# Attention with absorbed keys: eight heads stream past one batch's queries, in two column halves of the array

## The reference, cut to what matters

```python
x = x + attn(cond(x, subjects, weights, bias), WA, bA, ...)     # 64 batches x 64 tokens x 512
x = x + ffn(cond2(x, ...), Wg, bg, W1, W2)                      # 4 experts, top 2, unchanged

# cond: einsum('bct,bcd->bdt', x, weights[subject]) + bias[subject]
# attn, NH = 16 heads, DH = 128, DHR = 64, L = 128:
h = x @ WA + bA;  kv_lat, q_lat = split(h, 2)                    # 128 + 128 features
kRt = rope(h @ WB + bB);  qRt = rope(h @ WC + bC)                # 64 shared; 64 for each head
q, k, v = q_lat @ WUQ, kv_lat @ WUK, kv_lat @ WUV                # 128 for each head
scores = (q . k + qRt . kRt) * (128 + 64) ** -0.5, causal
out = softmax(scores) @ v @ WZ + bZ
```

## Time and profile before

| | |
|---|---|
| runs | 2027.82, 2028.1, 2031.16 us; median 2028.1 |
| profiled execution | span 2027.3 us from its first to its last instruction |
| start to the first attention matmul (weights absorbed) | 0 to 45.8 us |
| attention, eight groups | 45.8 to 1041 us |
| routing | to about 1269 us |
| experts | to the end |
| one group of attention, from one `bias_rows` to the next | 123.2 us (535.8 to 659.0) |

### The profile page before, as it was taken

How to read it: one execution, slowest core, us unless ns; L and a number is a source line. 1 busy time by engine, 2 the same in 40 slices (tenths; PEclk the granted TensorE clock), 3 DMA queues, 4 the chain that set the end, 5 groups by cost and what they waited for, 6 DMA issues and landing times. The chain is left out here.

```text
span 2027.3 us, 29249 instructions
## 1 busy us (share of the span) xinstructions
PE 1936.4 (96%) x10616; PEld 1601.5 (79%) x10616; DVE 944.1 (47%) x1604; ACT 627.5 (31%) x1088; POOL 735.3 (36%) x541
## 2 busy tenths in 40 slices
PE   6999999999999999999979997999999999999996
PEld 4788888888888888888867776787877878787875
DVE  4664656556475654747532386323323232323311
ACT  4323323233232323323212311333323333333321
POOL 2222222322223222232200003557565665657563
PEclk9999999999999999999989999899999999999998
DMA  6000101000010100101032212404312330322011
GB/s 244 21 1 16 47 0 62 0 32 30 0 62 0 62 0 0 62 0 63 1 83 93 94 68 71 168 0 128 88 32 41 124 78 5 103 98 47 0 21 21
DMA packets 68646, 104.88 MB, mean 52 GB/s; under 512 B 11904, under 2 KB 29056, under 8 KB 68608
## 3 DMA queue, kind: packets, MB, share of 16 engines
q1 hardware_dynamic: 49024, 77.69, 11.0%
q0 software_dynamic: 7168, 16.78, 4.3%
q10 hardware_dynamic: 12416, 9.88, 1.6%
HBM read 79.18 MB, written 25.17 MB: 51 GB/s over the span
## 5 line engine op out<-in xcount | busy, mean ns | idle before, releaser
L1721 DVE CAST hh<-hid 128x512 fp32r<-128x512 f32 x128 | 72.5, 567 | 483.0 <-ACT hid L1666 479.9
L396 POOL TENSOR_TENSOR rope_cos<-rope_raw,table_attend 128x512 f32<-128x512 f32 x72 | 93.2, 1295 | 454.2 <-ACT rope_raw L459 425.3
L1596 POOL TENSOR_TENSOR w1l<-w_raw,w1h 128x512 fp32r<-128x512 f32 x112 | 179.3, 1601 | 163.9 <-ACT w1h L1658 154.7
L95 PE MATMUL e_h<-xh,w1h 128*128 (+1 forms) x512 | 204.2, 399 | 14.8 <-POOL w1l L1596 13.4
L95 PE MATMUL bank_o<-Mh,mix_h 128*128 128x512 f32 x512 | 210.8, 412 | 0.0
L97 PE MATMUL e_h<-xh,w1l 128*128 (+1 forms) x512 | 202.5, 395 | 0.0
L96 PE MATMUL e_h<-xl,w1h 128*128 (+1 forms) x512 | 202.4, 395 | 0.0
L97 PE MATMUL bank_o<-Mh,mix_l 128*128 128x512 f32 x512 | 201.8, 394 | 0.0
L96 PE MATMUL bank_o<-Ml,mix_h 128*128 128x512 f32 x512 | 201.7, 394 | 0.0
L95 PE MATMUL e_y<-w2h,hh 128*128 128x512 f32 x512 | 200.1, 391 | 0.4 <-DVE hl L1723 0.4
L97 PE MATMUL e_y<-w2h,hl 128*128 128x512 f32 x512 | 199.3, 389 | 0.0
(11 more groups left out here) (297 smaller groups left out, 4047.6 us busy)
## 6 DMA issues: line engine op xcount, KB each, us to landing
w_raw<-in_W_dram SPq DMA_DIRECT2D x56, 512.0 KB, 4.2
stage<-in_x_dram SPq DMA_DIRECT2D x8, 1024.0 KB, 7.2
x_res<-in_x_dram SPq DMA_DIRECT2D x8, 1024.0 KB, 5.0
out_dram<-x_res SPq DMA_DIRECT2D x32, 256.0 KB, 2.0
flat_dram<-flat_sb ACTq DMA_DIRECT2D x32, 256.0 KB, 2.0
rows<-out_dram SPq DMA_DIRECT2D x4, 1024.0 KB, 5.5
x_odd<-out_dram SPq DMA_DIRECT2D x4, 1024.0 KB, 6.2
stage<-in_W_dram SPq DMA_DIRECT2D x8, 512.0 KB
```

Of the source, the lines that this page charges most:

```text
L95: nc.tensor.matmul(out, ah, bh, start=start and n == 0, stop=False)
L396: nc.gpsimd.tensor_tensor(by_cos[:, :].rearrange("p (b t) -> p b t", b=GB), v, cos.unsqueeze(1).to_broadcast([P, GB, C]), ALU.mult).then_i ...
L1596: nc.gpsimd.tensor_tensor(w1l[:, k, :, :], w1_at(pair, chunk), w1h[:, k, :, :].bitcast(F32), ALU.subtract).then_inc(S["w1_lo"], 1)
L1721: nc.vector.tensor_copy(hh[:, k, :], hid[:, k, :]).then_inc(S["h_hi"], 1)
```

## The change

A head's product with A now goes to the keys: `absorb_weights` computes A transposed (operands of L285 swapped), and `keys_absorbed` makes A kv_lat for every head, in place of `q_nope_mm` (3 matmuls for each of 16 heads in both). A **unit** `i` is now eight heads (`hb = i // 4`) of two batches (`n = i % 4`); there are eight units a group as before. In `scores` a batch's 64 queries are the stationary operand, and the absorbed keys of eight heads, 512 columns, stream past it; the two batches write partitions 0 to 63 and 64 to 127 of one bank, with stationary operands of 64 columns each. The keys' rope part is kept block-diagonal (`kblk`), for two heads at a time.

`mix` has four matmuls of 256 columns. `wz` of a unit is a closed sum over eight heads in one bank `bank_o`, so `x2_tile` adds to the residual once for each unit. The conditioning bias moves through the latent projection (`colsum`, `latent_bias`); the residual is stored and reloaded by quarters.

```diff
-                    nc.tensor.matmul(bank_s[:, cols], q_nope[:, b, :, :].rearrange("p h t -> p (h t)"),
-                                     lat32[:, 0, cols], start=b == 0, stop=False)
-                pe.wait_ge(S["rope_done"], g * NR + u + 2)
-                for b in range(GB):
-                    cols = slice(b * C, (b + 1) * C)
-                    last = nc.tensor.matmul(bank_s[:, cols], q_rope[:, b, :, :].rearrange("p h t -> p (h t)"),
-                                            k_rope[:, cols], start=False, stop=b == GB - 1)
...
+                half = [slice(j * C, (j + 1) * C) for j in range(2)]
+                tok = [slice((2 * n + j) * C, (2 * n + j + 1) * C) for j in range(2)]
+                for j in range(2):
+                    nc.tensor.matmul(bank_s[i % 2][half[j], :], q32[:, tok[j]], kabs[:, :, tok[j]],
+                                     start=True, stop=False)
+                for u in range(UB):
+                    for j in range(2):
+                        last = nc.tensor.matmul(bank_s[i % 2][half[j], u * P:(u + 1) * P], q_rope[:, u, tok[j]],
+                                                kblk[:, 2 * n + j, :, :].rearrange("p h t -> p (h t)"),
+                                                start=False, stop=u == UB - 1)
...
+                for j in range(2):
+                    for h in range(2):
+                        rows = slice(h * C, (h + 1) * C)
+                        toks = slice(j * C, (j + 1) * C)
+                        last[h] = nc.tensor.matmul(bank_m[h][:, :].rearrange("p (u q) -> p u q", u=UB)[:, :, toks],
+                                                   kv_tok[rows, (2 * n + j - h) % GB, :], probT[rows, :, toks],
+                                                   start=True, stop=True)
...
+            def wz(g, i, heads):
...
+                    if k == 0:
+                        pe.wait_ge(S["mix0_lo"], g * STEPS + i + 1)
+                        pe.wait_ge(S["x2_ev"], g * STEPS + i)
...
+            def keys_absorbed(g, h):
+                if h % HB < 2:
+                    pe.wait_ge(S["raw_ev"], g * NR + h // HB * UB + 4 + h % HB)
+                else:
+                    pe.wait_ge(S["ka_ev"], g * NH + h - 1)
...
+            def turn(r, sin):
+
+                dve.wait_ge(S["raw_ev"], r + 1)
+                dve.wait_ge(S["rope_done"], r)
+                nc.vector.memset(wait_here[:, :], 0.0)
+                nc.vector.stream_shuffle(swapped[:, :], raw[:, :], [i ^ 1 for i in range(32)]
+                                         ).then_inc(S["swap_ev"], 1)
...
+            def q_raw(g, u):
+                act.wait_ge(S["qr_mm"], g * NU + u + 1)
+                act.wait_ge(S["swap_ev"], g * NR + u + 1)
+                act.wait_ge(S["cos_ev"], g * NR + u + 1)
...
+            pe.wait_ge(wa_in, 16)
+            pe.wait_ge(t_ev["k"], HG)
+            for i in range(2):
+                for c in range(TC):
+                    last = nc.tensor.matmul(bank_t["k"][:, 2 * i:2 * i + 2], wa[:, c, i * L:(i + 1) * L],
+                                            K.parts["ones"][:, 0:2], start=c == 0, stop=c == TC - 1)
```

More of the change, by code:

```diff
@@ L330, in attention @@
[L330 to L337, removed]
+        lat_bias = (raw, swapped)
@@ L341, in attention @@
+        xres_in = K.xres_in
+        x2_out = [sem(f"at_x2_out{k}") for k in range(2)]
         block = ctx.enter_context(nc.Block())
@@ L449, in kv_tokens @@
[L449 to L451 removed]
+                nc.scalar.copy(lat_h[:, i, :], lat32[i]).then_inc(S["lat_hi"], 1)
+            def kv_tokens(g, k):
+                act.wait_ge(S["kvt_mm"], g * 2 + k + 1)
+                nc.scalar.copy(kv_tok[:, 4 * k:4 * k + 4, :], bank_p[k][:, :].rearrange("p (n l) -> p n l", n=4)
                                ).then_inc(S["kvt_ev"], 1)
[L454 to L459 removed]
@@ L520, in body @@
                         cond_hi(g + 1, c)
-                    latent(g + 1, 0)
-                    latent(g + 1, 1)
-                    kv_tokens(g + 1)
-                    rope_raw((g + 1) * NR, S["kb_mm"], g + 2, bank_d, K["bB"][:, 0:1])
+                    latent_hi(g + 1, 0)
+                prob_transposed(g, 6)
+                if more:
+                    latent_hi(g + 1, 1)
+                mix_hi(g, 6)
+                if more:
+                    keys_raw(g + 1)
+                    for u in range(UB):
+                        q_raw(g + 1, u)
+                    for h in range(HB):
+                        keys_absorbed(g + 1, h)
+                prob_transposed(g, 7)
+                if more:
+                    exps(g + 1, 0)
+                mix_hi(g, 7)
+                if more:
+                    kv_tokens(g + 1, 0)
+                    kv_tokens(g + 1, 1)
+                    exps(g + 1, 1)
             over_groups(act, first, body)
@@ L656, in first @@
                 latent_lo(0, 1)
[L657 to L683 removed]
+                keys_rope(0)
@@ new lines, in first @@
+            def first():
+                bias_rows(0, first=True)
+                for c in range(TC):
+                    cond(0, c, first=True)
+                latent(0, 0)
+                latent(0, 1)
+                rope_keys(0)
+                for u in range(UB):
+                    q_rope_mm(0, u)
+                for h in range(HB):
+                    keys_absorbed(0, h)
+                scores(0, 0, first=True)
+                scores(0, 1, first=True)
+                kv_tokens(0)
```

833 lines of the change are left out of this document (446 added, 387 removed).

## The result

The changed kernel takes 1979.0 us (median of 4 runs, 1978.1 to 1983.4) against 2028.0 (4 runs, 2027.4 to 2031.2) on the same chip: a ratio of 0.9757, 95% interval 0.9742 to 0.9771. It is faster, by 49 us where 67 were forecast: 2 us above the forecast of 1945 to 1977, and within the range given.

The account below looks back on a forecast made before the run. PE was taken as the bound, busy 122.3 of 123.2 us a group. Terms of -9.9 us a group gave -79 for eight; clock +7 and edges +5 made -67: 1961 us, forecast 1945 to 1977, range 1931 to 2012.

Parts of the forecast that it names:

- Scores, -12.3 a group: PE's f32 score matmuls: with column halves fully overlapped, 1.95 us a unit against 3.49, -12.3 us a group.
- The bound that the weight loads would add time: Score matmuls: 20 loads of 64 columns not hidden, 1.1 us a unit, 70 us in all: 2031; chance 0.04.
- The rival of a partial overlap: Score column halves overlap only in part, a pair costing 1.25 of one, +28 us: 1989; chance 0.12.
- The serial rival: Score column halves (L878, L882) run one after the other, +112 us less 16 of hidden waits: 2057; chance 0.12.
- Returns to fp32r, -1.2: First fp32r matmul behind f32 ones costs 0.32 instead of 0.23; about 14 a group, not 27: -1.2 us.
- Waits, +4.1 in sum: PE's waits a group: -0.8 us for old ones that go, +3.9 for a new one, +1.0 for others.
- The seam, +3.9: Front of a group: PE waits for `rope_raw` before `keys_absorbed` 1, a 12.8 us chain against 9.0 of matmuls: +3.9 us.
- Other waits, +1.0: Two or three PE waits of 0.52 us a group around `wz`, mix, scores or transposes: +1.0, from 0 to 4.
- Transposes, +0.4: Four more PE transposes a group for `kv_tokens`: +0.4 us.
- Clock, +7: New PE wait at seven group boundaries brings half clock behind some, 4 x 1.7 us: +7, from 0 to 12.
- Edges, +5: First group's front, without `wz` to fill and with a longer DVE chain, +4 us; end of `absorb_weights`, +1.
- The rivals of small and of long waits: PE waits: small, 1.8 us a group and clock holds, 1930, chance 0.15; long, 3 us more a group, 1990, chance 0.12.

Follow-up runs that it names:

- the run with the halves apart: Changed kernel with all five score matmuls of the first column half issued before those of the second: 2050.3 us, ratio 1.0094.
- the second buffer and all moved: Changed kernel with `rope_raw` doubled, scores kept in the probabilities' place, both reorderings, and unit 0's residual addition ahead of a DVE rope step: 1941.7 us, ratio 0.9570.
- both reorderings: Changed kernel with PE's and DVE's order changed at the front of a group, PE's and ACT's in its middle: 1955.2 us, ratio 0.9627.
- a second buffer: Changed kernel with `rope_raw` given a second buffer, used in turn, and scores kept in the probabilities' place: 2000.4 us, ratio 0.9858.
- DVE's line alone moved: Kernel with a second buffer, unit 5's residual addition moved ahead of two rope steps in DVE's queue, PE's order unchanged: 2003.5 us, ratio 0.9864.
- the middle alone mended: Changed kernel reordered only in mid-group: the mix of unit 2 moved ahead of `keys_absorbed` 9, ACT's copies likewise: 1969.0 us, ratio 0.9704.

## Why the prediction was right, and where it was off

- *Scores, -12.3 a group.* Right, and for the reason given. The bound that the weight loads would add time did not come: 20 records a unit pass in two slots of 0.43 and eight of 0.11, though both halves share their rows. The rival of a partial overlap falls too: a pair costs 1.0 of one. The Trainium skill ("TensorE: Matmul & The Clock Gate", Part 3) measured 2.38 for three column tiles; the estimate of 1.26 for a pair that the prediction worked out from it does not agree with this trace of two. The serial rival falls as well, and the run with the halves apart shows that it was a true one: at 1.7 times the time of a pair the kernel is 0.9% slower than before. In proportion (71 us for 0.71) the 49 us of the measured gain are gone at about 1.5; the 1.6 of the prediction belonged to a gain of 67.
- *Returns to fp32r, -1.2.* Right: there are 26 returns before and 14 after, each 0.09 longer than 0.23, so -1.1 is there. Entries into halves cost nothing new: the last fp32r matmul takes 0.33 ahead of halves six times a group now; before it was eight times, all ahead of the mix. That the row of the fp32r matmuls moves by only -0.1 comes from the waits.
- *Waits, +4.1 in sum.* **This is the term that was most undersized.** Idle time grew by 4.4, near the forecast. But each of the four waits costs 0.27 more in the matmuls on its two sides, and two short stops under 0.15 us that the view does not list (527.07 to 527.74, 544.80 to 545.52) cost another 0.45 together: 1.5 us a group, against 0.5 ahead of the three waits of before. So waits are +5.4. A kernel with half as many such stops bears it out: with the second buffer and all moved, the fp32r matmuls without waits are 76.2 us a group instead of 77.0.
- *The seam, +3.9.* The forecast came from a chain of 12.8 us. The chain took 13.3 (from 523.14, where the keys' matmuls are through, to 536.44), so PE, with 9.0 us of its own to issue, lost 4.3, of which 3.4 are listed as idle, in three stretches instead of one or two. The 0.5 more is in the two additions for the keys: 2.39 us instead of 1.9, the second beside POOL's product of 527.43.
- *Other waits, +1.0.* The fourth wait, of 1.91 us in the middle of the group, was in no term by name; the 1.0 us were placed at mix, scores or `wz`. There ACT's copy (581.74) comes when POOL's cosine product ends, at 581.65, behind POOL's division and residual bias (578.24, 1.73 us). But DVE's shuffle, for which it waits too, ended only at 581.42. So POOL's order is worth little there, and moving the residual bias, in the kernel with both reorderings, gave nothing.
- *Transposes, +0.4.* Undersized: +1.2. The four more for `kv_tokens` are +0.5. The other +0.7 is in the sets directly ahead of the scores' halves, four a group, which take up to 0.58 instead of 0.36. The prediction had seen an entry cost in the mix and charged it to the scores alone. Waits and transposes together are 2.1 us a group, 17 us in eight, and smaller terms give 2 back: those are the 15 us by which the groups fell short. Half clock is another 6.6 of the 21 that are missing between the spans (67 forecast, 45.8 measured).
- *"Residual addition in DVE's queue".* Right as a mechanism, and of more weight than it was given: its place decides whether a second buffer loses 21 us or gains.
- *Clock, +7.* Right in kind, half the size: 13.6 us. Five stretches stand at seams, where four were forecast. The three in the middle were not foreseen, as the wait there was not, and the front of the first group has two in place of one longer one before.
- *Edges, +5.* What is left for them is +6.3 in attention, less 1.7 behind it. Only the 1.6 ahead of the first group (forecast 1) was measured by itself.
- *No change in routing and experts.* Right, within 2 us.
- The rivals of small and of long waits did not come as they were told. The first, at 1930, is what the edits of the order approach (1942 at best). The time of 1979 lies above the forecast of 1977 and was in the range by the room that was kept for rivals near 1990, which were wrong or came only in part: the mechanism was right, and its losses were sized too small.

## What to carry to other kernels

When small matmuls are put side by side in column halves, issue them alternately: the same ten matmuls took 1.9 us in turn and 3.2 us one half after the other, and here that is the difference between 2.4% faster and 0.9% slower. Count what stands at the borders between full and half width, as well as what stands within.

After such a change the next loss is in the queues. A second buffer alone made it worse, since it let one engine run ahead into a wait behind another's queue; look for every place where the addition that frees a bank stands behind work that is not yet needed, not for the first one only. Of two fixes that a wait suggests, try the order of the queue before the buffer: it costs no memory and here gave as much. Move both ends of the wait, though: with DVE's line alone moved, DVE waited for PE instead.

## What was not expected of the hardware

- Matmuls of one column half did not wait for all of the other's in the queue ahead of them: with the halves apart, the second half's first one started at 582.26, with three records of the first half still to start. Every unit of that run shows this order.
- DVE's rope products and POOL's products do not slow one another by a share: the second waits for the first. Wherever a rope product of DVE starts while one of POOL's instructions runs, it ends 0.55 us after POOL's, however long that still took (all 73 cases in attention of the changed kernel): that of 524.92 ends at 527.12, POOL's at 526.58. DVE's product of 128x512 takes 0.69 us alone (530.56), so beside POOL it takes anything up to 2.20. When DVE starts first it is the other way round: DVE's takes 0.69 as if alone (531.29), and POOL's cosine product ends 1.12 to 1.16 us after it (56 cases; 531.33 takes 1.81, against 1.30 when POOL starts first). This is why the mean of 1056 ns says little: which of the two starts first sets the price. Timeline of DVE, then of POOL, at the seam of the changed kernel:

```profile
524.92 2.20 DVE L638 TENSOR_TENSOR rope_swapped<-rope_swapped,table_attend 128x512 f32<-128x512 f32 x1
...
530.56 0.69 DVE L638 TENSOR_TENSOR rope_swapped<-rope_swapped,table_attend 128x512 f32<-128x512 f32 x1
531.29 0.69 DVE L657 TENSOR_TENSOR q_rope<-q_rope,rope_swapped 128x512 f32<-128x512 f32 x1
```

```profile
524.17 2.41 POOL L416 TENSOR_TENSOR k_blocks<-rope_raw,table_attend 128x1024 f32<-128x1024 f32 x1 [16.86 <-ACT rope_raw L500]
...
531.33 1.81 POOL L424 TENSOR_TENSOR q_rope<-rope_raw,table_attend 128x512 f32<-128x512 f32 x1 [2.33 <-ACT rope_raw L507]
```

- The half clock does not follow the sum of the waits. In the profiled execution with the middle alone mended, PE still waited 38 us in attention and the clock fell twice; in that of the changed kernel, with 44 us, it fell ten times. These are counts of one execution each. Which wait brings it about stays open.
